# Delta rule: products of levels 0 to 4 and the diagonal on 32-column tiles

## The reference

```python
def step(s, inp):
    qt, kt, vt, at, bt = inp
    s = s * at[..., None]
    u = jnp.einsum('bhd,bhdv->bhv', kt, s)
    s = s + bt[..., None, None] * (kt[..., None] * (vt - u)[..., None, :])
    out = jnp.einsum('bhdv,bhd->bhv', s, qt)
    return (s, out)
```

## Time and profile before

| | us |
|---|---|
| median of 3 runs | 5169.21 |
| lowest, highest | 5156.3, 5171.2 |
| span of the profiled execution | 5145.8 |
| TensorE busy, of the span | 3922.1 |
| span of the delta loop in it | 2404 |

### The profile page before, as it was taken

The page is one execution under the profiler, slowest core; times in us unless marked ns, Lnnn a source line. Parts: engine busy times, 40 slices in busy tenths (PEclk is TensorE's granted clock), DMA queues, the critical chain, the costliest instruction groups (busy, mean ns, idle before and its releaser), DMA issues. The chain is left out here.

```text
span 5145.8 us, 181702 instructions
## 1 busy us (share of the span) xinstructions
PE 3922.1 (76%) x73332; PEld 3131.2 (61%) x73332; DVE 2953.6 (57%) x8172; ACT 1773.9 (34%) x4061; POOL 2629.7 (51%) x3000
## 2 busy tenths in 40 slices
PE   4779973674068888888888888888886679588695
PEld 2534443664047676766677676767674479477595
DVE  5832267755556665656556566656555645488723
ACT  3732231442023333333333333333333134211163
POOL 2310016514546666666666666666664242477644
PEclk8989986886579999999999999999998889799797
DMA  0030003664000000000000000000000056200154
GB/s 22 2 138 0 0 3 95 190 181 121 23 15 14 11 14 11 14 11 14 11 11 14 11 14 11 14 11 14 11 14 8 18 208 229 87 1 1 61 187 125
DMA packets 129703, 249.33 MB, mean 48 GB/s; under 512 B 24672, under 2 KB 60656, under 8 KB 127344
## 3 DMA queue, kind: packets, MB, share of 16 engines
q1 hardware_dynamic: 98224, 178.93, 11.0%
q0 software_dynamic: 16384, 33.59, 2.2%
q10 hardware_dynamic: 14400, 26.22, 1.4%
HBM read 178.89 MB, written 59.77 MB: 46 GB/s over the span
## 5 line engine op out<-in xcount | busy, mean ns | idle before, releaser
L2597 POOL TENSOR_TENSOR e_kd<-e_kd,e_tail 128x512 f32<-128x512 f32 x325 | 368.9, 1135 | 587.2 <-PE psum L2709 586.7
L2739 PE MATMUL psum<-e_T,e_N 64*64 64x32 f32 x10400 | 402.3, 228 | 71.3 <-remote 34.8
L2739 PEld LDWEIGHTS psum<-e_T,e_N 64*64 64x64 f32 x10400 | 363.3, 141 | 100.7 <-issue 99.7
L2709 PE MATMUL psum<-e_kd,e_k 64*64 64x64 f32 x10400 | 396.7, 228 | 28.6 <-DVE e_AT L3127 28.4
L729 POOL DMA_INDIRECT m_back<-m_rows_out,m_idx x256 | 253.3, 990 | 295.8 <-DVEq L1169 121.5
L2709 PEld LDWEIGHTS psum<-e_kd,e_k 64*64 64x64 f32 x10400 | 361.2, 143 | 37.3 <-issue 37.1
L3133 DVE COPY e_Z<-psum 64x256 f32<-64x256 f32 x325 | 135.8, 418 | 386.0 <-PE psum L2739 384.2
L3022 ACT ACTIVATE e_T<-psum 128x256 f32<-128x256 f32 x325 | 125.9, 387 | 631.1 <-PE psum L2760 631.1
L723 POOL DMA_INDIRECT rows_in<-xn,m_idx x256 | 256.0, 1000 | 145.5 <-issue 76.2
L840 PE MATMUL psum<-m_rowsT,m_w 128*128 128x128 f32 x2304 | 317.3, 297 | 3.0 <-DVE m_h L1145 2.3
L2760 PE MATMUL psum<-e_Z,e_TT 64*64 64x32 f32 x8320 | 297.6, 222 | 26.7 <-DVE e_Z L3133 21.2
(11 more groups left out here) (464 smaller groups left out, 10744.4 us busy)
## 6 DMA issues: line engine op xcount, KB each, us to landing
m_w<-in_m_w SPq DMA_DIRECT2D x88, 516.0 KB, 5.7
m_w<-in_m_w SPq DMA_DIRECT2D x224, 129.0 KB
m_rows<-rows_in SPq DMA_DIRECT2D x100, 256.0 KB, 3.8
m_rows_out<-m_out ACTq DMA_DIRECT2D x100, 256.0 KB, 2.1
m_w<-in_m_w SPq DMA_DIRECT2D x88, 259.0 KB, 3.6
e_w<-in_e_w SPq DMA_DIRECT2D x66, 321.0 KB, 3.0
rows_in<-xn SPq DMA_DIRECT2D x6, 2048.0 KB, 23.4
m_wd<-in_m_wd SPq DMA_DIRECT2D x3, 2048.0 KB, 8.1
```

Source lines behind the costliest of these rows:

```text
L2597: return g.tensor_tensor(both_odd(dst[:], m), both_odd(src[:], m), gate.unsqueeze(1).broadcast_to((P, 2, nb, m)), ALU.mult)
L2709: r = pe.matmul(c.psum[half(h), G_, chunk(u)], keys[half(h), chunk(u)], both_odd(gated[half(h), :, chunk(u)], 1 << l), start=True, stop=True)
L2739: r = pe.matmul(c.psum[half(1 - h), Z_, u * HC:(u + 1) * HC], N[half(h), l - 1, chunk(u)], even(T[half(h), chunk(u)], 1 << l), start=True, ...
```

## The change

Two slices are added, `rows_of(h, b)` for the 32 partitions of block b of head h, and `tokens(u, b)` for the 32 tokens of block b of chunk u. The diagonal, gram products of levels 0 to 4, Z and T products of levels 1 to 4 are made for each of the two 32-token blocks by itself, and the blocks off the diagonal are left out. The diagonal and gram products contract over the head's 64 rows and have 32 output partitions (64 x 32 tiles); Z and T contract over 32 rows and have 32 output partitions (32 x 32 tiles). Each product moves half as many columns as before, and there are twice as many. Level 5 of Z, T and gram is as before, and so is the order of blocks and the alternation of Z and gram by chunk.

```diff
--- before.py
+++ after.py
@@ -2545,6 +2545,12 @@
     def block(t):
         return slice(t * P, (t + 1) * P)
 
+    def rows_of(h, b):
+        return slice(h * DH + b * HC, h * DH + (b + 1) * HC)
+
+    def tokens(u, b):
+        return slice(u * CH + b * HC, u * CH + (b + 1) * HC)
+
     def odd(ap, m):
         return ap.rearrange("p (b c) -> p b c", c=2 * m)[:, :, m:2 * m]
 
@@ -2698,17 +2704,42 @@
                 pe.wait_ge(ket_ready, 1)
                 pe.sem_clear(ket_ready)
                 for u in range(NC):
+                    for b in range(2):
+                        for h in range(2):
+                            r = pe.matmul(c.psum[rows_of(h, b), X_, tokens(u, b)], kn[half(h), tokens(u, b)],
+                                          kqn[half(h), 1, tokens(u, b)], start=True, stop=True)
+                r.then_inc(d_ps, 1)
+
+            def gram_chunk(l, keys, gated, u):
+
+                if l + 1 == LEVELS:
                     for h in range(2):
-                        r = pe.matmul(c.psum[half(h), X_, chunk(u)], kn[half(h), chunk(u)], kqn[half(h), 1, chunk(u)],
-                                      start=True, stop=True)
-                r.then_inc(d_ps, 1)
-
-            def gram_chunk(l, keys, gated, u):
-
-                for h in range(2):
-                    r = pe.matmul(c.psum[half(h), G_, chunk(u)], keys[half(h), chunk(u)],
-                                  both_odd(gated[half(h), :, chunk(u)], 1 << l), start=True, stop=True)
+                        r = pe.matmul(c.psum[half(h), G_, chunk(u)], keys[half(h), chunk(u)],
+                                      both_odd(gated[half(h), :, chunk(u)], 1 << l), start=True, stop=True)
+                    return r
+                for b in range(2):
+                    for h in range(2):
+                        to = c.psum[rows_of(h, b), G_, chunk(u)].rearrange("p (n c) -> p n c", n=2)
+                        r = pe.matmul(to[:, :, b * HC // 2:(b + 1) * HC // 2], keys[half(h), tokens(u, b)],
+                                      both_odd(gated[half(h), :, tokens(u, b)], 1 << l), start=True, stop=True)
                 return r
+
+            def z_chunk(l, u):
+
+                if l + 1 == LEVELS:
+                    for h in range(2):
+                        r = pe.matmul(c.psum[half(1 - h), Z_, u * HC:(u + 1) * HC], N[half(h), l - 1, chunk(u)],
+                                      even(T[half(h), chunk(u)], 1 << l), start=True, stop=True)
+                        if u + 1 == NC:
+                            r.then_inc(z_ps[h], 1)
+                    return
+                for b in range(2):
+                    for h in range(2):
+                        at = u * HC + b * HC // 2
+                        r = pe.matmul(c.psum[rows_of(1 - h, b), Z_, at:at + HC // 2], N[rows_of(h, b), l - 1, tokens(u, b)],
+                                      even(T[rows_of(h, b), tokens(u, b)], 1 << l), start=True, stop=True)
+                        if u + 1 == NC and b == 1:
+                            r.then_inc(z_ps[h], 1)
 
             def gram(l, keys, gated, free, done):
                 pe.wait_ge(free, 1)
@@ -2735,11 +2766,7 @@
                 pe.wait_ge(gr_free, 1)
                 pe.sem_clear(gr_free)
                 for u in range(NC):
-                    for h in range(2):
-                        r = pe.matmul(c.psum[half(1 - h), Z_, u * HC:(u + 1) * HC], N[half(h), l - 1, chunk(u)],
-                                      even(T[half(h), chunk(u)], 1 << l), start=True, stop=True)
-                        if u + 1 == NC:
-                            r.then_inc(z_ps[h], 1)
+                    z_chunk(l, u)
                     if l + 1 < LEVELS:
                         r = gram_chunk(l + 1, k, kd, u)
                     elif u % 2:
@@ -2756,9 +2783,16 @@
                     pe.sem_clear(tt_ready)
                 left = (TT0, TT, TT, TT, TTH)[l - 1]
                 for u in range(NC):
-                    for h in range(2):
-                        r = pe.matmul(even(c.psum[half(h), T_, chunk(u)], 1 << l), left[half(h), chunk(u)], Z[half(h), u, :],
-                                      start=False, stop=False, skip_group_check=True)
+                    if l + 1 == LEVELS:
+                        for h in range(2):
+                            r = pe.matmul(even(c.psum[half(h), T_, chunk(u)], 1 << l), left[half(h), chunk(u)], Z[half(h), u, :],
+                                          start=False, stop=False, skip_group_check=True)
+                        continue
+                    for b in range(2):
+                        for h in range(2):
+                            r = pe.matmul(even(c.psum[rows_of(h, b), T_, tokens(u, b)], 1 << l), left[rows_of(h, b), tokens(u, b)],
+                                          Z[rows_of(h, b), u, b * HC // 2:(b + 1) * HC // 2],
+                                          start=False, stop=False, skip_group_check=True)
                 r.then_inc(t_ps, 1)
 
             def cross_z():
```

## The result

The changed kernel takes 6193.1 us (median of 4; 6186.4 to 6201.4) against 5162.8 for the kernel before: a ratio of the fast runs of 1.2007, 95% interval 1.1985 to 1.2029. It is 20% slower; 5819 was forecast, with a range of 5450 to 6260.

A forecast was written before the change was run, and what follows sets the result against it. TensorE (PE), busy 87% of the delta loop, was taken as the bound. Profiled span 5145.8 + 455 (7.0 us x 65 iterations) + 195 (clock) = 5796, with 23.4 up to the median 5819 us; range 5450 to 6260.

The forecast's parts named there:

- The sign: Whole kernel: slower, with chance 0.86.
- (a): Seven blocks (gram 0, diagonal, gram 1, T 1 to 4): 0.67 us instead of 0.96, gaining 2.2 us an iteration.
- the entry price: Six of the seven pure blocks newly begin with a shape change, 0.10 us each: 0.6 us an iteration back.
- (b): Z-and-gram blocks, levels 1 to 4: 16 shape changes make 3.04 us; 8.1 us an iteration lost, 0.4 for entries.
- The rival in which tiles on disjoint parts of the array don't drain: Z-and-gram blocks run on as now, only overlapping tiles delay: 1.2 us less an iteration, 5091 us; chance 0.13.
- (c): PE's waits in the loop absorb little: about 0.4 us hidden, 0.5 us of gains lost, nearly cancelling.
- The balance of 7.0 us an iteration: Delta loop before clock effects: 8.1 + 0.4 + 0.6 - 2.2 + 0.1 = 7.0 us, x 65 = 455 us.
- (d): Delta loop: 6 us more an iteration at 1.2 GHz, 0.5 us lost each, 195 us; clock about 0.90.
- the clock that stays: Delta loop: drains as forecast but the clock stays where it is, 5624 us; chance 0.27.
- Narrow tiles that load no faster: Pure blocks remain at 0.96 us, 2.2 us an iteration not gained, 143 us on top, 5962 us; chance 0.05.

The follow-up runs named there:

- run 3: Kernel before with only diagonal, gram 0, gram 1 and T 1 to 4 narrow, Z and other grams as before: 5390.3 us, ratio 1.0460.
- run 11: Kernel before with, in levels 1 to 4, Z products of all chunks first, then gram, all on 64x64 tiles: ratio 1.0038.
- run 12: Kernel before with, in levels 1 to 4, gram products of all chunks first, then Z, all on 64x64 tiles: ratio 1.0337.
- run 4: Kernel before with only Z 1 to 4 and gram 2 to 4 narrow and alternating in shape: 6046.4 us, ratio 1.1733.
- run 9: Kernel of run 5, but Z of levels 1 to 3 contracts over 32 rows, so Z and gram alternate in shape: ratio 1.0612.
- run 5: Kernel before on narrow tiles with no more instructions: only the first 32-token block of each head and chunk made, the other left out; ratio 0.9910.
- run 1: Changed kernel with Z of levels 1 to 3 over 64 rows and level 4 at 64x64, no shape change inside Z-and-gram blocks: 5769.95 us, ratio 1.1200.
- run 2: Changed kernel with, in levels 1 to 4, all Z products first, then all gram, 2 shape changes instead of 16: 5830.5 us, ratio 1.1308.
- run 6: Kernel before with only T 1 to 4 narrow (32x32), 128 records more an iteration: ratio 1.0192.
- run 7: Kernel of run 1 with TensorE's loop written out once instead of 13 times: ratio 1.1618.
- run 8: Changed kernel with Z and gram alternating every two chunks, 8 shape changes a block instead of 16: ratio 1.1453.
- run 10: Kernel before with gram 0, gram 1, diagonal and keys' transposition each issued twice on wide tiles: ratio 1.0390.

## Why the prediction was right or wrong

The sign, the mechanism and the range held; the point forecast of +656 us was 374 us too low. By steps:

**(a), the pure blocks:** 0.67 us forecast, 0.66 measured for T, with the entry price. But only where the instructions came; the gain of 2.2 us an iteration was more than undone, as run 3 with its breaks shows: 1.6 us less forecast, 3.6 us more measured. I had looked at 64 such records in another stage and not asked whether a whole iteration of them can be supplied. That is the term that was missing.

**(b), the alternation:** groups at 0.19 us forecast, 0.18 and 0.19 measured; the block 3.04 forecast, 3.00 measured for levels 1 to 3 and 3.53 for level 4, whose wide gram groups take 0.26. The rival in which tiles on disjoint parts of the array don't drain is refuted by the same rows: they are disjoint, and each group starts 0.07 or 0.08 us before the end of the last. The Trainium skill, TensorEngine Tiling (Array Packing), section Key Properties, which has the drain at every change of mode, agrees.

**(c), what hides:** little, as said, for this order of work; runs 11 and 12 show that it would be otherwise with Z first. The balance of 7.0 us an iteration can be compared with run 4, which has all of the drains and next to no breaks. Its part of the sum is 8.1 + 0.4 = 8.5 us; it measures 13.4, the rest with a clock of 0.80.

**(d), the clock:** the right sign, and the wrong size. I took 6 us more an iteration at 1.2 GHz and a clock of 0.90; it was 25.5 us more (28.4 after, 2.9 before) and 0.73. The price for each was too high, 0.5 us per us. In run 4, 4.9 us are left beyond its 8.5 for 17.3 us more at 1.2 GHz: 0.28. The blocks of the changed kernel say the same: an alternating one takes 3.00 us at 2.4 GHz and 3.95 at 1.2, which is 0.24 lost per us at 1.2, a narrow T block 0.66 and 1.01, which is 0.35; a wide T block of run 4 takes 1.05 and 1.83, 0.43. With run 4's 0.28 the changed kernel is 7.0 (work) + 25.5 x 0.28 = 7.1 (clock) + 1.9 (breaks, 2.3 less 0.4) = 16.0 us an iteration; measured are 53.2 - 37.1 = 16.1. The split between clock and breaks rests on run 4's price and on breaks counted in full, so it is an estimate; that each exists alone is shown by runs 4 and 9 (drains and low clock without breaks) and run 3 (breaks and low clock with few drains). So two errors of (d) worked against each other: four times as much low clock as forecast, at about half the price. That the range held owes something to this. The iteration grew by 16.1 us and not by 10.0; 4.1 of the difference are the clock and 1.9 the breaks, for which the sum had no term.

**The rivals:** the clock that stays is refuted (0.73). In run 9 the clock fell with groups 0.2 us apart and no long gap added: from 1700 to 3700 us TensorE has 4 idle gaps over 1 us, in run 5 it has 31. The Trainium skill, TensorE: Matmul & The Clock Gate, section Why this matters for your kernels, warns of idle gaps between bursts of matmuls; by that alone run 9 would not have lost clock, so it doesn't carry over to this case. Narrow tiles that load no faster are refuted by 0.66 us.

**The breaks** are a wait for instructions. Runs 1 to 10 already say so: loads and matmuls stop together with no semaphore, the packets of the instruction queue grow with the instructions, the number alone doesn't bring breaks (run 10) and narrow tiles alone don't (run 5), both together do (runs 1, 2, 3, 6). The packets themselves, whose times are in the same traces, settle it. Queue q8 brings 16 KB at a time, and 230 packets more came for 58,240 more loads and matmuls, so one packet holds about 256 instructions. The four breaks shown above end at 2826.82, 2838.73, 2529.31 and 2520.04 us; the last packets before them had landed at 2825.25, 2837.24, 2528.02 and 2518.70. The packet ahead of run 1's break (2529.31) is the only one from 2526.50 to 2529.32 us:

```profile
q8 instruction: 1, 0.02, 2.6%
```

Of all 1613 breaks in the loops of the 14 kernels each ends between 1.17 and 1.61 us after a packet has landed; of instants taken at random in the same loops only 9 to 12 in 100 lie so. From one packet to the next it is 4.0 us in the median of run 1, and only 2 in 100 of its packets follow within 3.4 us, though a narrow block uses up a packet in about a microsecond. An estimate from that: an iteration of the changed kernel needs 11 packets, and 11 x 3.4 is 37 us, as long as the whole iteration of the kernel before. By that, this many instructions had next to nothing to win even without a drain. Why packets do not follow faster is open.

## What to carry to other kernels

Before making tiles smaller, count the changes of tile shape that the written order gives, and price each at the drain that the trace shows at its other borders: a saving of a few tenths of a microsecond per block is gone after three of them. Then ask for the rate at which the instructions would have to come: divide the loads and matmuls of an iteration by 256, and compare with the time between instruction packets that the trace shows. Halving the work of each instruction and doubling their number helps only if a row shows that rate held over more than one block. And where a change adds drains or halts to TensorE, allow for time at 1.2 GHz, and price it block by block: a block that mostly drains lost 0.24 us per us of it, a wide one 0.43.

## What the runs showed of the hardware

- A change of tile shape holds TensorE until 0.07 us before the modelled end of the last matmul even when the old and the new tiles share no part of the array, with four records between changes as with eight (0.18 to 0.24 us a group).
- Blocks of narrow f32 products, about 9 ns a record, break off for about 1 us with matmuls and weight loads; 6.6 us an iteration in run 1, 0.4 us where the same number of instructions is spent on wide tiles (run 10, against 1.7 in run 6).
- TensorE's instructions come in packets of 16 KB, about 256 instructions each, in run 1 a median of 4.0 us apart and seldom under 3.4; each of the 1613 breaks ends 1.17 to 1.61 us after one has landed.
- A turn of the hardware loop halts TensorE for about 3 us (run 7: 39 turns, 121.8 us). Written out once instead of 13 times the loop fetched more packets (888 against 809) and took 4.6 us an iteration longer.
- The clock was at 1.2 GHz for more than half of the loop of the changed kernel though matmul records covered 92% of it; in the kernel before they covered 87% with the clock at 0.96.
